# Last turn's steps grouped two and six instead of four and four, with two products of the last block but one between the groups

## The reference

```python
x = _layernorm(x + _L1_gnn_ref(x, ..., edge_type_8, W, root, bias))     # pass 1
x = _layernorm(x + _L2_gnn_ref(x, ..., weight, comp, attn..., update))  # pass 2
x = _layernorm(x + _L3_gnn_ref(x, W, bias_term, gates..., loop_weight)) # pass 3

# pass 1, per relation r:
hr = x @ W[r]
msg = hr[src] * mask[:, None]
s = jax.ops.segment_sum(msg, dst, num_segments=n_nodes)
out = out + s / jnp.maximum(c, 1.0)[:, None]
# pass 2: srcs = alphas[rels] * srcs_dense[rels, src]; vrps.at[dst].add(srcs)
# pass 3: msg = xw[rel, src] + bias_term[rel]; summed with a gate at dst
```

## Time and profile before

| what | value |
|---|---|
| runs, us | 2488.3, 2485.68, 2489.79 (median 2488.3) |
| the profiled execution | 2488.5 us, of which span 2486.7 us |
| PE busy | 1431.5 us (58%) |
| POOL busy | 1366.1 us (55%) |
| DVE busy | 935.5 us (38%) |
| ACT busy | 633.0 us (25%) |
| gathers, L809 | 1248, 990 ns each, 1235.4 us |
| mean granted TensorE clock | 0.756 |

### The profile page before, as it was taken

How to read it: one execution, slowest core, us unless ns; L and a number is a source line. 1 busy time by engine, 2 the same in 40 slices (tenths; PEclk the granted TensorE clock), 3 DMA queues, 4 the chain that set the end, 5 groups by cost and what they waited for, 6 DMA issues and landing times.

```text
span 2486.7 us, 30099 instructions
## 1 busy us (share of the span) xinstructions
PE 1431.5 (58%) x6376; PEld 930.2 (37%) x6481; DVE 935.5 (38%) x2464; ACT 633.0 (25%) x1671; POOL 1366.1 (55%) x1541
## 2 busy tenths in 40 slices
PE   4666699999988065655556165554454333343343
PEld 3333345445444053444434043433333233332333
DVE  6999622122116943223322443333333222212222
ACT  0677400000013043333333154434444000000000
POOL 1000025220211877777775677777776577777776
PEclk7888899999999587666776586667766666656556
DMA  0000001000026133333333222222222222222221
GB/s 20 0 0 0 18 14 12 6 5 1 6 49 257 37 105 102 92 105 105 106 105 96 72 78 74 71 76 76 76 75 64 65 55 55 54 54 55 55 54 46
DMA packets 120619, 148.87 MB, mean 60 GB/s; under 512 B 74779, under 2 KB 88737, under 8 KB 117362
## 3 DMA queue, kind: packets, MB, share of 16 engines
q0 software_dynamic: 40000, 81.89, 12.6%
q1 hardware_dynamic: 80562, 66.31, 8.2%
HBM read 91.39 MB, written 56.72 MB: 60 GB/s over the span
## 4 chain that ended last, share of the span: by engine, by line
POOL 45%; PE 26%; issue 17%; DVE 6%; ACT 4%; DMA 1%; POOLq 1%; SPq 0%; ACTq 0%; DVEq 0%
POOL adj L809 45%; PE acc L1053 16%; PE acc L944 4%; PE acc L1136 2%; ACT adj L1307 1%; ACT acc L1311 1%; PE acc L1200 1%; PE misc L988 1%; ACT adj L1386 1%; PE acc L1166 1%; DMA adj<-table,adj 1%; DVE feat L1605 0%; DVE adj L1936 0%; DMA table<-adj 0%; DVE adj L1971 0%
## 5 line engine op out<-in xcount | busy, mean ns | idle before, releaser
L809 POOL DMA_INDIRECT adj<-table,adj x1248 | 1235.4, 990 | 443.8 <-issue 377.9
L1200 PE MATMUL acc<-adj 128*128 x2640 | 526.8, 375 | 720.1 <-ACT adj L1386 347.5
L1200 PEld LDWEIGHTS acc<-adj 128*128 128x128 f32 x2640 | 474.9, 276 | 786.7 <-issue 786.3
L1592 DVE TENSOR_TENSOR adj<-node_iob,drel 128x384 f32<-128x384 bf16 (+1 forms) x444 | 226.3, 552 | 617.8 <-PE acc L1200 616.3
L1386 ACT ACTIVATE adj<-adj 128x128 f32<-128x128 f32 x832 | 263.1, 389 | 584.5 <-DMA adj<-table,adj 500.4
L1053 PE MATMUL acc<-adj,feat 128*128 (+2 forms) x2042 | 400.2, 353 | 6.4 <-DVEq L1641 3.3
L759 POOL TENSOR_TENSOR node_rep<-node_rep,compb 128x128 f32<-128x128 f32 x128 | 58.2, 455 | 548.0 <-DMA node_rep<-in_L_gnn_weight_dram 539.2
L1053 PEld LDWEIGHTS acc<-adj,feat 128*128 (+1 forms) x2100 | 185.6, 98 | 212.3 <-DVEq L1641 3.4
L1166 PE MATMUL acc<-adj 128*128 128x512 f32 (+1 forms) x350 | 199.1, 715 | 72.2 <-ACT adj L1401 72.2
L944 PE MATMUL acc<-feat 128*128 128x400 bf16 x625 | 142.1, 387 | 78.2 <-ACT acc L1311 68.9
L1605 DVE TENSOR_SCALAR feat<-feat 128x400 bf16<-128x400 int16 x625 | 156.9, 322 | 0.0
(11 more groups left out here) (264 smaller groups left out, 1011.4 us busy)
## 6 DMA issues: line engine op xcount, KB each, us to landing
table<-adj SPq DMA_DIRECT2D x50, 512.0 KB, 2.8
table<-adj SPq DMA_DIRECT2D x25, 1024.0 KB, 4.3
adj<-table,adj POOLq DMA_INDIRECT x1250, 2.5
table<-adj SPq DMA_DIRECT2D x25, 64.0 KB, 1.6
temp<-in_x_dram SPq DMA_DIRECT2D x6, 256.0 KB, 3.2
out_dram<-adj SPq DMA_DIRECT2D x24, 64.0 KB, 1.6
wrel<-node_rep SPq DMA_DIRECT2D x16, 64.0 KB, 3.0
adj<-in_L_gnn_W_dram SPq DMA_DIRECT2D x2, 512.0 KB, 5.2
```

Source lines behind the costliest of these rows:

```text
L809: pool.indirect_dma_start(ring[:, p_, 0:D], None, table, bass.IndirectOffsetOnAxis(ap=gidx[:, p_:p_ + 1], axis=0)).then_inc(msgs_in[u.r][c ...
L1200: last = nc.tensor.matmul(acc[:, bass.ds(blk[s], width)], hot[:, c, j, :], ring_flat[:, bass.ds(place[s], width)], start=False, stop=True, ...
L1592: return nc.vector.tensor_tensor(o, node_iob[:, :].unsqueeze(1).to_broadcast([P, n, P]), drel[:, bass.ds(s, n)].unsqueeze(2).to_broadcast( ...
```

## The change

The constants of the last turn become a pair, `LAST = (2, 6)`: group 0 has two steps and group 1 six. The other edits:

```diff
-LASTG, LASTNB = 4, 2
+LAST = (2, 6)
+LASTNB = len(LAST)
+BEFORE_LAST = 2
...
-            return [LASTG] * LASTNB if t.last() else [G] * NB
+            return list(LAST) if t.last() else [G] * NB
...
-            nc.gpsimd.memset(edge_i[0:1, 0, STEPS - LASTG + SPT - G:WSTEPS], BLOCKS - 1).then_inc(off_set, 1)
+            nc.gpsimd.memset(edge_i[0:1, 0, STEPS - LAST[1] + SPT - G:WSTEPS], BLOCKS - 1).then_inc(off_set, 1)
...
-            def products(ph, b):
+            def products(ph, b, which=slice(None)):
...
-                for j, o, table in parts:
+                for j, o, table in parts[which]:
...
-                        landed(t, 1)
+                        if not t.last():
+                            landed(t, 1)
                     elif c == 1:
-                        if not t.last():
-                            landed(t, 2)
+                        landed(t, 1 if t.last() else 2)
...
-                        if c == 1 and made:
+                        if c == (0 if t.last() else 1) and made:
                             transposed(ph, b)
+                            if t.last():
+                                products(ph, b, slice(0, BEFORE_LAST))
...
-                        products(ph, b)
+                        products(ph, b, slice(BEFORE_LAST if t.last() and not general else 0, None))
...
-                    take(ph, t, 1)
+                    if not t.last():
+                        take(ph, t, 1)
...
                         if ph < 3:
                             features(ph, b)
+                        take(ph, t, 1)
                         return
...
-            nc.vector.tensor_scalar(walk_i[0:1, TURNS - 1, WAITS:WAITS + LASTNB], ...
+            for c in range(LASTNB):
+                end = WHOLE + sum(LAST[:c + 1])
+                nc.vector.tensor_scalar(walk_i[0:1, TURNS - 1, WAITS + c:WAITS + c + 1], ts_f[0:1, end - 1:end], 1.0, None, ALU.add)
```

More of the change, by code:

```diff
@@ L88 @@
 assert TQ * TC == TILES and NI * QB == BLOCKS and TURNS == BLOCKS and (BLOCKS - 1) * P < NA <= NP
-assert (TURNS - 1) * SPT + LASTG * LASTNB == STEPS and (TURNS - 1) * TPT + SIZES[0] + SIZES[1] == TILES
+assert (TURNS - 1) * SPT + sum(LAST) == STEPS and (TURNS - 1) * TPT + SIZES[0] + SIZES[1] == TILES
 assert 2 * KB + D + 1 <= BANK3 * KB and TURNS % AHEAD_T == 1
@@ L787, in body @@
                                                     ).then_inc(gmsgs_in[c], 16)
-                        of_c = (TURNS - 1) * G + (LASTG if c < LASTNB else 0)
+                        of_c = (TURNS - 1) * G + (LAST[c] if c < LASTNB else 0)
                         hold(pool, gmsgs_in[c], z * (16 * of_c) + t.num(16 * G, 16 * n))
@@ L1532, in _ @@
                                     ts_f[0:1, 0:WHOLE].rearrange("p (i q j) -> p i q j", i=TURNS - 1, q=NB)[:, :, :, G - 1], 1.0, None, ALU.add)
-            nc.vector.tensor_scalar(walk_i[0:1, TURNS - 1, WAITS:WAITS + LASTNB],
-                                    ts_f[0:1, WHOLE:STEPS].rearrange("p (q j) -> p q j", q=LASTNB)[:, :, LASTG - 1], 1.0, None, ALU.add)
+            for c in range(LASTNB):
+                end = WHOLE + sum(LAST[:c + 1])
+                nc.vector.tensor_scalar(walk_i[0:1, TURNS - 1, WAITS + c:WAITS + c + 1], ts_f[0:1, end - 1:end], 1.0, None, ALU.add)
             nc.vector.tensor_scalar(turn_i[0:1, 0, :], bs_f[0:1, :], 21846.0, None, ALU.mult)
```

## The result

The changed kernel takes 2496.12 us (median of 22 runs, 2485.65 to 2500.28), the kernel before 2488.19 us (22 runs, 2482.71 to 2495.11). The ratio is 1.0029, 95% interval 1.0021 to 1.0038: slower by 7.2 us, between 5.2 and 9.5. The forecast was +6.8 us.

The account below looks back on a forecast made before the run. POOL's gathers set the pace, and only the ends of the three passes change: 4.8 + 3.9 - 1.9 = +6.8 us on 2488.5, so 2495.3, say 2495.0 us as median; range 2489.5 to 2498.

Parts of the forecast that it names:

- Pass 1, +4.8 forecast: End of pass 1: block 24's transposition 3.1 us later, plus 1.7 us for PE's low clock; +3.1 if the clock stays up.
- The term from one transposition to the other: Pass 1: block 23's transposition at 1363.3 and block 24's at 1373.8, in place of 1363.49 and 1370.72.
- The clock term: Pass 1, PE's last products: a gap of some 3 us brings the low clock, costing 1.7 us; the least certain term.
- Pass 2, +3.9 forecast: End of pass 2: block 24's transposition at 1936.6 in place of 1932.72, +3.9 us, between +3.1 and +4.6.
- The gain at the start: Pass 2: ACT's take moves behind the sigmoid, so DVE's wait for it goes; 0.15 us gained.
- the clock costs nothing there: Pass 2, behind block 24's transposition: ACT's table load and sigmoid and DVE set the pace, not PE; 0 us.
- Pass 3, -1.9 forecast: End of pass 3: group 0 runs before the last gather lands, block 24 summed at 2479.4 in place of 2481.26; -1.9 us.
- the clock rival: Rival: PE's clock stays up over pass 1's gap; +5.1 us in all, 2493.5 us; chance 0.19.
- The clock stays up: Rival for pass 1: no low clock behind the gap, +3.1 there, +5.1 us in all, 2493.5 us; chance 0.19.
- PE alone decides: Rival: block 24's norm costs DVE nothing, only group 1 is added to PE's row; +0.6 us, 2489; chance 0.12.
- The gain of pass 3 in all passes: Rival: block 23 done before the last tiles arrive in every pass, -1.9 us three times, 2482.6 us; chance 0.06.
- The general program: Case: the bound for it is missed and the whole kernel is slower by far more than any range; 1 in 100.

Follow-up runs that it names:

- E3: Changed kernel plus ten matmuls of zeros in PE's idle stretch ahead of block 24's transposition in pass 1; ratio to the kernel before 1.0020.
- E2b: The same kernel as E2, run again on another chip; ratio to the kernel before 0.9992.
- E2: Changed kernel with PE's and ACT's order of before put back, groups of two and six and pass 3's freed wait kept; ratio to the kernel before 1.0004.
- E7: Kernel before with pass 3's needless wait freed and ACT's take of the last tiles behind the sigmoid in pass 2; ratio 0.9975.
- E6: Changed kernel with groups of four and four in place of two and six, interleaved order kept; ratio to the kernel before 1.0010.
- E4: Changed kernel with all of block 23's products ahead of the last group in place of two; ratio to the kernel before 1.0057.
- E8: E7 with pass 1's side product first, block 24's transposition between block 23's products, and pass 2's sigmoid of block 23 earlier; ratio to the kernel before 0.9975.
- E1: Kernel before with one edit: pass 3's first group of the last turn no longer waits for the last four gathers; ratio 1.0005.
- E2c: The same kernel as E2, run again on a third chip to see pass 3 undisturbed; ratio to the kernel before 0.9998.

## Why the prediction was right

**Pass 1, +4.8 forecast, +3.9 measured.** The term from one transposition to the other was forecast as 10.5 us and was 10.11; before 7.23. DVE's copies took 1.68 us up to the transposition and not 1.88, its sum and norm 2.59 and not 2.71, and group 1 ended 0.1 us sooner than I had it. The clock term was forecast as 1.7 us and was 1.69 (E3 against the changed kernel). The start came 0.6 us earlier (9.72 us from the last gather to the transposition of block 23, 10.35 before) and not 0.2. Of this, 0.28 stood already at the start of group 0, by a faster clock over the products of block 22 (6.41 and 6.69 us from the last gather); the other 0.35 is the shorter group 0, which I had at 0.2. Over executions the clock's terms vary (E2b against E2: 1.7 us), so a single profile is good to about that.

**Pass 2, +3.9 forecast, +4.35 measured.** Three terms were mis-sized, and they cancel in part. The gain at the start was 1.1 us (8.91 us from the last gather to the transposition, 10.01 before), forecast as 0.15. Most of it is not the change's: PE's products of block 22 were 0.75 us faster in this execution (2.97 us, 3.72 before, shown below), and L1838 waits for them, as I had it. E7, whose products took 3.69 us, puts the moved take by itself at 0.3 us; I had 0.15 because I counted from the end of L1838's 0.69 us, while in E7 L1845's work starts 0.61 us behind the start of L1838's. Between the transpositions it was +4.5 and not +4.0, group 1 being at the low clock almost to its end (2.61 us, where I took 2.2 out of 1.4 to 2.9). And "the clock costs nothing there" was wrong: DVE waited 0.51 us for the last product. The write of the last rows took 3.18 us to land, 2.87 before. The products of block 22, changed kernel and before:

```profile
1923.41 2.97 PE L1168 MATMUL acc<-adj 128*128 128x136 f32 x6
```

```profile
1920.79 3.72 PE L1166 MATMUL acc<-adj 128*128 128x136 f32 x6
```

**Pass 3, -1.9 forecast, -1.5 measured.** The mechanism held; the six steps took 2.92 us at 0.49 us each, where I had taken 0.435 from the sixteen records of before.

**The sum.** The mechanism is shown, but that the tails add up to the forecast 6.8 us to a tenth is luck: the three passes were off by -0.9, +0.45 and +0.4. The clock term of 1.7 us is luck in part as well. I held a gap of some 3 us to be enough for the low clock; in the changed kernel it was, and in E6, with a gap shorter by 0.25 us, it was not. The interval of the 22 runs, 5.2 to 9.5, reaches down almost to the clock rival's +5.1.

**The rivals.** "The clock stays up" did not happen in the profile, though it did in E6's; E3 shows its price. "PE alone decides" is out by E4. "The gain of pass 3 in all passes" did not come, since group 0 of pass 1 was not held up by the last tiles: it ran behind the products of block 22 without a wait (1361.19 us, above). The general program did not run: the changed kernel makes the same number of gathers and steps (x1248 and x2640 in both profiles).

## What to carry to other kernels

Where two engines work through a tail by turns, an instruction that sits in an idle stretch of one of them is free only as long as what it feeds is not needed later on the other: ask which queue its result releases before putting anything ahead of it. Here the reordering cost 3.9 and 4.35 us in two passes, while freeing a needless wait and moving one step of ACT, with PE's order left alone (E7), gained 6.2 us (3.2 to 9.0). And read a change at a program's serial ends between fixed points of the timeline: differences of 0.5 us showed there that 22 runs of the whole program cannot tell. But read the granted clock of each stretch beside them, since one total (E6, pass 1) came out near the forecast for another reason than the one given, and another (E8, pass 2) hid a gain of 1.2 us.

## What the runs showed of the hardware

- The clock that PE is granted at a pass's end is worth 1.7 us for three products, and it differs between executions of the same code (4.54 and 2.85 us, E2 and E2b, which ran on two chips; on one chip and in the same code, the products of block 22 in pass 2, 3.69 us in E7 and 2.88 in E8). With matmuls of zeros in the idle stretch it was up in all three profiled executions (2.85, 2.21 and 2.21 us for three products). Idle stretches of 1.71 and 0.37 us with a transposition between them in before, and of 1.35 and 0.37 us in E2, were followed by the low level; the same 1.35 and 0.37 us in E2b by the full one. Ahead of block 24's products, 2.46 and 0.37 us in the changed kernel were followed by the low level, 2.21 and 0.37 us in E6 by the full one. So the outcome of gaps of that size is not fixed by them.
- Three of four chips ran the same program 10% slower, with pauses of PE, DVE and ACT together of some 15 us, while matmuls, copies and writes between the pauses took what they take elsewhere (from the transposition of block 24 to the next gather in pass 1, 9.83 or 9.84 us in E1, E2, E2b and E2c, 9.83 before). What these pauses are is open.
